# Softplus rounds interleaved with the chunks that turn u, and dt*u in four pieces, in a selective scan

## What is computed

```
dts = softplus(dt_projs_w @ dts + dt_projs_b)
dA  = exp(dt_t[..., None] * As)
h   = h * dA + (dt_t * u_t)[..., None] * B_t
y_t = sum over the 16 states of h * C_t
```

## Time and profile before

| | |
|---|---|
| median of 3 runs | 1604.85 us (1603.81 to 1606.59) |
| the profiled execution | 1609.95 us, span of its instructions 1608.2 us |
| the scan's units in it | 189.5 us to about 1313 us |
| busy in the span: TensorE, VectorE, ScalarE, GpSimd | 84%, 77%, 63%, 64% |
| mean granted TensorE clock | 0.95 of full speed |

### The profile page before, as it was taken

How to read it: one execution, slowest core, us unless ns; L and a number is a source line. 1 busy time by engine, 2 the same in 40 slices (tenths; PEclk the granted TensorE clock), 3 DMA queues, 4 the chain that set the end, 5 groups by cost and what they waited for, 6 DMA issues and landing times. The chain is left out here.

```text
span 1608.2 us, 66443 instructions
## 1 busy us (share of the span) xinstructions
PE 1351.8 (84%) x30424; PEld 829.6 (52%) x30424; DVE 1232.1 (77%) x1025; ACT 1011.7 (63%) x1916; POOL 1025.0 (64%) x294
## 2 busy tenths in 40 slices
PE   6997679788987878888797898879787967879998
PEld 6744455454554545455464555545454533436554
DVE  4876199989798899989889998997998985742220
ACT  2458677787678778777777867777776630412222
POOL 0002089899798989989898998988899860000000
PEclk7898889999999999999999999999999987889999
DMA  9243514334233433323343342334324225101101
GB/s 322 94 155 144 169 55 112 83 84 98 68 80 88 112 76 92 99 68 91 77 112 88 80 111 70 79 75 112 94 73 127 65 79 225 40 0 40 40 35 44
DMA packets 73478, 151.08 MB, mean 94 GB/s; under 512 B 33238, under 2 KB 41942, under 8 KB 72816
## 3 DMA queue, kind: packets, MB, share of 16 engines
q1 hardware_dynamic: 73200, 146.83, 31.5%
HBM read 101.72 MB, written 32.51 MB: 83 GB/s over the span
## 5 line engine op out<-in xcount | busy, mean ns | idle before, releaser
L1213 POOL TENSOR_TENSOR s_h<-s_h,s_crow 128x2048 f32<-128x2048 f32 (+1 forms) x256 | 878.9, 3464 | 160.1 <-DVE s_h L1178 159.9
L1178 DVE TENSOR_TENSOR_SCAN s_h<-s_a,s_pb 128x1024 f32<-128x1024 f32 x384 | 864.2, 2276 | 138.4 <-PE s_pb L1006 103.1
L1006 PE MATMUL s_pb<-k_area,m_dtut 64*64 64x64 f32 x24576 | 470.9, 224 | 163.9 <-DVE s_h L1178 112.4
L1006 PEld LDWEIGHTS s_pb<-k_area,m_dtut 64*64 64x64 f32 x24576 | 426.6, 138 | 342.9 <-DVE s_h L1178 159.0
L1047 PE MATMUL s_py<-s_h,k_eye 64*64 64x512 f32 x3072 | 421.4, 604 | 16.4 <-issue 6.6
L286 ACT ACTIVATE k_area<-k_mask,m_bt 128x64 f32<-128x64 f32 x992 | 274.0, 338 | 0.0
L1104 ACT ACTIVATE s_a<-m_dup,m_aneg 128x1024 f32<-128x1024 f32 x192 | 219.4, 1143 | 28.9 <-DVE s_h L1178 28.8
L201 POOL TENSOR_TENSOR k_area<-m_bt,k_mask 128x2048 f32<-128x2048 f32 x33 | 145.7, 4418 | 129.9 <-ACT m_bt L264 129.9
L1104 ACT ACTIVATE s_a<-y_y,m_aneg 128x1024 f32<-128x1024 f32 x192 | 218.3, 1138 | 10.1 <-DVE s_h L1178 10.0
L264 ACT COPY y_y<-m_pm 128x384 f32<-128x384 f32 (+1 forms) x96 | 49.2, 513 | 104.0 <-PE m_pm L221 92.6
L1047 PEld LDWEIGHTS s_py<-s_h,k_eye 64*64 64x64 f32 x3072 | 91.9, 136 | 34.5 <-issue 23.1
(11 more groups left out here) (189 smaller groups left out, 1237.0 us busy)
## 6 DMA issues: line engine op xcount, KB each, us to landing
s_crow<-scratch_xd SPq DMA_DIRECT2D x256, 256.0 KB, 4.1
k_area<-in_x_dram SPq DMA_DIRECT2D x4, 1536.0 KB, 7.8
scratch_xt<-y_y SPq DMA_DIRECT2D x4, 1536.0 KB, 8.7
y_y<-y_y SPq DMA_DIRECT2D x24, 256.0 KB, 3.3
m_dup<-m_dup SPq DMA_DIRECT2D x24, 256.0 KB, 3.8
out_dram<-t_out SPq DMA_DIRECT2D x32, 192.0 KB, 1.9
k_area<-scratch_xt SPq DMA_DIRECT2D x3, 1536.0 KB, 6.8
scratch_xd<-h_dbl SPq DMA_DIRECT2D x8, 512.0 KB, 2.6
```

The costliest lines, as they stand in the source:

```text
L1006: mm = pe.matmul(pb[par * HALF:(par + 1) * HALF, step % 2, r * BANK + blk:(r + 1) * BANK:BLK], dtut[here, u % 2, blk, g * HALF:(g + 1) * H ...
L1178: nc.vector.tensor_tensor_scan(h[:, step % (TRIPLES * CG), f], a[:, step % RING, f], pb[:, step % 2, f], 0.0, ALU.mult, ALU.add).then_inc( ...
L1213: nc.gpsimd.tensor_tensor(here, here, c.unsqueeze(1).broadcast_to([P, groups.stop - groups.start, L]), ALU.mult).then_inc(hc_ready, 1)
```

## The change

The three rounds of softplus begin at steps 7, 10 and 13. Where u is turned, its four chunks stand at steps 7, 10, 13 and 15, each but the first after the round before it; a logarithm waits until the chunk in front of it is taken from `m_pm`. dt*u is made in four pieces of 384 columns, after the scans of steps 18 to 21. Where a new sum of y begins late, in the even units, it begins at step 9 in place of 8, two steps behind the other units, and catches up at steps 10 and 13 (at both, two steps are added). The six pieces that carry the sum are at steps 11, 12, 14 and 15 of the same unit and at steps 8 and 11 of the next. The load of u for the skip moves from n = 5 to n = 6 in SyncE's queue.

```diff
-CAUGHT_UP = 9
-CARRIED = 6
+BEHIND = {LAG: 1, LAG + 1: 2, LAG + 2: 2, LAG + 3: 1, LAG + 4: 1, LAG + 5: 1}
+CARRIES = {(2, 11): 0, (2, 12): 1, (2, 14): 2, (2, 15): 3, (3, 8): 4, (3, 11): 5}
+ROUND_AT = (7, 10, 13)
+TIMES_AT = 18
+QUARTERS = 4
...
-    return {"Z": 0, "BT": 4, "UT": 5, "DUP": 16}[what] + i
+    return {"Z": (0, 1, 2, 3), "BT": (4,), "UT": (7, 10, 13, 15), "DUP": (16, 17, 18, 19)}[what][i]
...
         if what == "UT":
+            if u:
+                need(pe, self.dt_ready, ROUNDS * u + i)
...
-    def times_u(self, dve, u):
-
+    def times_u(self, dve, u, quarters):
+
+        blocks = slice(quarters.start * BLK // QUARTERS, quarters.stop * BLK // QUARTERS)
         dve.wait_ge(self.dt_ready, ROUNDS * (u + 1))
         dve.wait_ge(self.chunk_taken, CHUNK[u - u % 2, "UT", 3] + 1)
         need(dve, self.b_row, STEPS * (u - 1))
-        self.nc.vector.tensor_tensor(self.dtut[:, u % 2].rearrange("p k c -> p (k c)"), self.zs, self.ut[:].rearrange("p k c -> p (k c)"),
-                                     ALU.mult).then_inc(self.dtu_ready, 1)
+        self.nc.vector.tensor_tensor(self.dtut[:, u % 2, blocks].rearrange("p k c -> p (k c)"),
+                                     self.dt_of[:, blocks].rearrange("p k c -> p (k c)"), self.ut[:, blocks].rearrange("p k c -> p (k c)"),
+                                     ALU.mult).then_inc(self.dtu_ready, len(quarters))
...
-                    if n == 5 and s == 1 and o == 0:
+                    if n == 6 and s == 1 and o == 0:
                         sp.wait_ge(chunk_done, CHUNK[u + 1, "UT", 3] + 1)
                         load_u(sp, d, keep, shared, b, "skip")
...
-            def carry(b, piece):
-
-                first = CG * NP * 4 * b + CG * NP * 2
-                pe.wait_ge(y_added, first + CAUGHT_UP + 2 + piece - LAG)
+            def carry(b, piece, made):
+
+                pe.wait_ge(y_added, made)
...
-            def sums(u, i):
...
+            def summed(u, i):
+
                 held = u > 0 and u % 2 == 0
...
+                return max(0, u * STEPS + i + 1 - LAG - (BEHIND.get(i, 0) if held else 0))
...
-                    for summed in sums(u, i):
-                        add_y(summed // CG, summed % CG)
-                    if u % 4 == 2 and CAUGHT_UP < i <= CAUGHT_UP + CARRIED:
-                        carry(u // 4, i - CAUGHT_UP - 1)
+                    made = summed(u, i)
+                    for at in range(summed(u, i - 1), made):
+                        add_y(at // CG, at % CG)
+                    if (u % 4, i) in CARRIES:
+                        carry(u // 4, CARRIES[u % 4, i], made)
...
             def logarithm(u, r):
                 act.wait_ge(exp_ready, u + 1)
-                act.wait_ge(chunk_taken, CHUNK[u, "DUP", 0])
+                act.wait_ge(chunk_taken, CHUNK[u, "BT", 0] + 1 + (r + 1 if u % 2 == 0 else 0))
...
-                        if i in (9, 11, 13):
-                            logarithm(u + 1, (i - 9) // 2)
+                        if i in ROUND_AT:
+                            logarithm(u + 1, ROUND_AT.index(i))
...
-                        if 9 <= i < 15:
-                            softplus(u + 1, (i - 9) // 2, (i - 9) % 2 * 2)
-                            softplus(u + 1, (i - 9) // 2, (i - 9) % 2 * 2 + 1)
-                        if i == 15:
-                            m.times_u(dve, u + 1)
+                        for r, at in enumerate(ROUND_AT):
+                            if at <= i < at + 2:
+                                softplus(u + 1, r, 2 * (i - at))
+                                softplus(u + 1, r, 2 * (i - at) + 1)
+                        if TIMES_AT <= i < TIMES_AT + QUARTERS:
+                            m.times_u(dve, u + 1, range(i - TIMES_AT, i - TIMES_AT + 1))
```

More of the change, by code:

```diff
@@ L247, in take_chunk @@
         if what == "Z":
-            need(act, self.dtu_ready, u)
+            need(act, self.dtu_ready, QUARTERS * u)
             need(act, self.dt_ready, ROUNDS * u)
@@ L881, in _ @@
             nc.vector.scalar_tensor_tensor(zs, zs, 0.0, lnz, ALU.max, ALU.add).then_inc(m.dt_ready, ROUNDS)
-            m.times_u(dve, 0)
+            m.times_u(dve, 0, range(QUARTERS))
         @block.gpsimd
@@ L973, in _ @@
                         sp.wait_ge(y_stored[0], 2 * Y_STORED)
-                        sp.wait_ge(dtu_ready, UNITS)
+                        sp.wait_ge(dtu_ready, QUARTERS * UNITS)
                         sp.wait_ge(dt_ready, ROUNDS * UNITS)
@@ L996, in spread_b @@
                 if i == 0:
-                    pe.wait_ge(dtu_ready, u + 1)
+                    pe.wait_ge(dtu_ready, QUARTERS * (u + 1))
                 if i % 6 == 0:
@@ L1026, in carry @@
                 mm.then_inc(y_carried, 1)
-                pe.wait_ge(y_carried, CARRIED * b + piece + 1)
+                pe.wait_ge(y_carried, len(CARRIES) * b + piece + 1)
             def add_y(n, part):
@@ L1048, in add_y @@
                 mm.then_inc(y_added, 1)
-            def sums(u, i):
-                at = u * STEPS + i - LAG
+            def summed(u, i):
                 held = u > 0 and u % 2 == 0
-                if at < 0 or held and i == LAG:
-                    return []
-                if held and LAG < i < CAUGHT_UP:
-                    return [at - 1]
-                if held and i == CAUGHT_UP:
-                    return [at - 1, at]
-                return [at]
+                return max(0, u * STEPS + i + 1 - LAG - (BEHIND.get(i, 0) if held else 0))
             for u in range(UNITS):
@@ L1107, in take_y @@
                 act.wait_ge(y_added, CG * NP * 4 * (b + 1))
-                act.wait_ge(y_carried, CARRIED * (b + 1))
+                act.wait_ge(y_carried, len(CARRIES) * (b + 1))
                 nc.scalar.copy(y01[:].rearrange("p (h w) -> p h w", w=HW), py[:].rearrange("p (w h) -> p h w", h=HW)).then_inc(y_taken, 1)
```

## The result

The changed kernel takes 1655.3 us (median of 6 runs, 1647.62 to 1660.86), the kernel before beside it on the same chip 1606.7 us (6 runs, 1603.81 to 1618.27): the ratio is **1.0287, 95% interval 1.0245 to 1.0329**. The forecast of 1649 us against 1604.85 is a ratio of 1.0275, inside the interval. The profiled execution spans 1653.6 us against 1608.2, so 45.4 us more.

What follows compares the result with a forecast made beforehand. No engine alone bounds the kernel; what counts is who waits for whom, step by step. Terms -1.3 (turning u), +49.5 (pieces of dt*u) and -4 (stalls) make +44 on 1604.85: 1649 us, range 1625 to 1682.

Steps and rivals of the forecast that it cites:

- the main term: Steps 18 to 21: dt*u pieces blocked by GpSimd's products, +3.3 us x 15 units = +49.5 us.
- Part 2: dt*u in four pieces at steps 18 to 21: each waits for a whole GpSimd instruction, +49.5 us in all.
- the meeting of unit 4: Steps 18 to 21: worked-out times of pieces against GpSimd's products; scan 22 starts 28.0 us after scan 13's start.
- Rival 2: Steps 18 to 21: GpSimd's products of h with C don't block VectorE; 1606 us, chance 0.09.
- Part 3: The rest, chiefly TensorE late at steps 16 to 18 by the fourth chunk of u: hidden, nothing added.
- the first piece is ready at 16.9, still before 17.4: hidden: Step 18, units turning u, from scan 13's start: piece ready before GpSimd's long product ends at 17.4, so lateness costs nothing.
- the sentence on the lost cover: Step 18, units turning u: if the long product no longer hides TensorE's lateness, 1.0 us x 7 = +7 us.
- Rival 1: From step 18: first piece misses the seam, second waits for the long product; 1664 us, in all units 1682; chance 0.13.
- The gain by stalls: Steps 22 to 24: TensorE, no longer behind, swallows part of its stalls; -4 us, between 0 and -10.
- Part 1: Turning u moved out of steps 5 to 8: ScalarE's late logarithm limits the gain; -1.3 us in all.
- Rival 3: Steps 5 to 8: TensorE is the real bound, logarithm not late, pieces slip into GpSimd's pauses; 1585 us, chance 0.10.

Runs made afterwards that it cites:

- e3: The changed kernel with each dt*u piece after the first unit replaced by a bn_stats over the same columns, one SBUF input: 1631.09 us, ratio 1.0121.
- e2: The kernel before with only dt*u cut into four pieces at steps 18 to 21: 1631.03 us, ratio 1.0117.
- e1: The changed kernel with dt*u whole again, after the scan of step 15, or 16 where u is turned: 1636.43 us, ratio 1.0158.
- e6: The changed kernel with the fourth chunk of u at step 16 and the copies of dt a step later: 1634.19 us, ratio 1.0132.
- e12: The kernel before plus two useless one-SBUF-input bn_stats on VectorE after each of scans 18 to 21: 1627.2 us, ratio 1.0126.
- e7: The changed kernel with ScalarE's expansions of B moved out of steps 4 to 8: 1628.05 us, ratio 1.0091.
- e4: The kernel before with the chunks of u at steps 8, 9, 11 and 13, dt*u whole at step 15: 1645.81 us, ratio 1.0202.
- e8: The kernel before with whole dt*u at step 15 or 19, later softplus rounds and u chunks in odd units, B expansions outside steps 4 to 8: 1629.01 us, ratio 1.0088.
- e10: e8 with the load of the next unit's rows ahead of the doubling of dt on SP's queue, all rows built: 1605.44 us, ratio 0.9955.

## Why the prediction was right

The sign, the place and the mechanism of the main term held. The other three were mis-sized, and that their errors nearly cancel is luck.

- **Part 2, that one of them blocks the other for the whole instruction**: right, and for GpSimd's h times C as well, which no row of before showed. e3 and the softplus operations show that the second SBUF input is the cause. +49.5 us forecast, +48.0 in e2; the meeting of unit 4 comes within 0.2 us of the working. Rival 2 falls.
- **Part 3, "TensorE is late by about 0.4, 0.3 and 0.3 us at steps 16 to 18"**: this is the step that failed. Measured are 1.58, 0.55 and 0.31 us. I priced the chunk and its wait at the upper clock; behind 2.85 us without work the granted clock is 0.57, and chunk and spread take 1.62 + 1.99 us. With the clock at 1.00 behind the same pause (e1, unit 3) the scan of step 16 waits 0.37 us, as forecast. So "the first piece is ready at 16.9, still before 17.4: hidden" was 18.51 against 17.87. The lateness then counts in full, as the sentence on the lost cover says, but it is 2.9 us a unit and not 1.0: +20 us for its +7 (e6). Rival 1 is not what happens, though the first piece does miss the seam and 30.68 is near its 30.2: its second piece waits for a long product, and here it takes 0.52 us.
- **The gain by stalls, "estimate 0.3 us x 14 = -4 us, between 0 and -10"**: measured -31.8 us, outside its bounds: -18.4 from T(22) to the next T(0), about where it was forecast, and -13.4 in steps 0 to 4, which the forecast leaves out. I read two stalls off two units, and let TensorE catch up only in part; e2 and e12 show that 3 us a unit of time that VectorE spends on its own take 28 us out of the 305 in those steps.
- **Part 1, -1.3 us**: +4.1. The even units are right (+1.6 and +3.0 forecast, 204.5 - 199.2 = +5.3 measured). In the odd units the wait for the logarithm is 2.83 us for the 2.6 forecast, at the place named; but T(5) to T(13) gains 1.1 us there and not 5.9. The second chunk, at step 10, is slow for the same reason as the fourth: the wait for the first logarithm lets TensorE stand still for 3.75 us, the granted clock over the 3.5 us behind it is 0.55, and the second logarithm is 0.41 us late in unit 5. e7 shows that ScalarE's queue was the cause of the first wait. Rival 3 falls by its own test: 9.5 us after T(5), but with a wait in front.

What the issue gaps in TensorE's weight loads are made of, no run here shows; nor why they are 142.7 us in e12 and 96.7 in the kernel after. That 3 us of VectorE's own work ahead of the seam cover them, without any blocking by GpSimd, is what e12 shows.

## What to carry to other kernels

Before an operation with two SBUF inputs on VectorE is moved or cut up, write down which GpSimd instruction will be running at each of its new starts, to the tenth of a microsecond: 0.5 us of work cost 0.5 or 2.7 us here, and in e4 a lateness of 0.6 us made 4.7 us out of 1.7. A wait put on TensorE is priced with the slower clock behind it, as behind the pauses of 2.8 and 3.75 us here, or it is moved to where what it waits for is over: one step later no scan waited (e6), and the same distance of two steps cost some 17 us in e8 and in e10. And when a step gets longer, look for the stalls of the other engine that it covers, before adding it to the sum: of the 48 us of the pieces alone 28 came back.
